# Perceiver block on one core: the last chunk of the cross attention gets a ring of five exp banks

## What is computed

```python
x = x + xattn(layernorm(x), ctx)          # the change is at the end of this one
x = x + attn(layernorm(x))                # 16 heads of 64
x = x + ffn(layernorm(x))                 # 16 experts, 4 chosen, and a shared one

def xattn(q, c, w_q, w_kv, w_concat):
    qh = (q @ w_q).reshape(B, L, 16, 16).transpose(0, 2, 1, 3)
    k, v = split(c @ w_kv)
    p = softmax(einsum('bhid,bjd->bhij', qh, k) / 4)
    return merge_heads(einsum('bhij,bjd->bhid', p, v)) @ w_concat
```

## Time and profile before

| | |
|---|---|
| median of 3 runs | 604.72 us (599.29 to 612.70) |
| the profiled execution | 603.77 us, of which the profile's span is 602.0 us |
| granted TensorE clock, mean | 0.99 |
| TensorE, VectorE, ScalarE, GpSimd busy | 93%, 77%, 67%, 20% of the span |
| where the last chunk lies | scores of its first tiles at 372.36 us, the product behind its loop at 395.50 us |

### The profile page before, as it was taken

The page is one execution under the profiler, slowest core; times in us unless marked ns, Lnnn a source line. Parts: engine busy times, 40 slices in busy tenths (PEclk is TensorE's granted clock), DMA queues, the critical chain, the costliest instruction groups (busy, mean ns, idle before and its releaser), DMA issues.

```text
span 602.0 us, 11657 instructions
## 1 busy us (share of the span) xinstructions
PE 558.3 (93%) x4488; PEld 301.6 (50%) x4488; DVE 464.7 (77%) x683; ACT 400.8 (67%) x814; POOL 121.9 (20%) x158
## 2 busy tenths in 40 slices
PE   2788999999999999999999999898999987989996
PEld 0353343344334433433443343356766765968885
DVE  5797997999999999999999994615445558695565
ACT  1326887888888888888888888753556553335441
POOL 5000000000000000000000000402366552177852
PEclk9989999999999999999999999998999999899999
DMA  8864200000122100000000000100050030032101
GB/s 314 216 121 127 79 25 25 25 26 26 34 52 69 44 1 1 1 2 2 1 2 2 1 1 1 36 2 17 19 175 28 10 105 2 1 97 88 50 5 35
DMA packets 19482, 28.09 MB, mean 47 GB/s; under 512 B 5570, under 2 KB 13316, under 8 KB 18404
## 3 DMA queue, kind: packets, MB, share of 16 engines
q1 hardware_dynamic: 19428, 27.35, 16.1%
HBM read 20.78 MB, written 0.52 MB: 35 GB/s over the span
## 4 chain that ended last, share of the span: by engine, by line
PE 73%; DVE 19%; ACT 3%; issue 3%; DMA 2%; SPq 0%; DVEq 0%
PE bank L658 23%; PE bank L669 19%; DVE mxp L1232 11%; PE pairS L747 5%; PE pairS L911 5%; PE bank L929 3%; PE pairS L797 3%; PE bank L824 2%; PE bank L911 2%; PE bank L810 2%; DMA ctx<-ctxT 2%; ACT Pb L1024 2%; PE bank L601 2%; PE pairS L677 1%; DVE Pb L1314 1%
## 5 line engine op out<-in xcount | busy, mean ns | idle before, releaser
L1232 DVE TENSOR_REDUCE mxp<-pairS 128x1 f32<-128x1024 f32 x256 | 308.2, 1222 | 20.3 <-PE pairS L652 19.2
L1024 ACT ACTIVATE Pb<-bank 128x512 f32<-128x512 f32 x512 | 278.2, 597 | 47.1 <-PE bank L658 23.8
L658 PE MATMUL bank<-qparts,kparts 64*128 64x512 f32 x512 | 184.2, 447 | 9.2 <-DVE mxp L1232 2.9
L652 PE MATMUL pairS<-kparts,qparts 64*128 64x512 f32 x512 | 183.5, 451 | 4.5 <-DVE mxp L1232 3.4
L669 PE MATMUL bank<-Pb,V 128*32 128x256 f32 x2048 | 160.3, 390 | 1.2 <-ACT accS L1010 1.2
L658 PEld LDWEIGHTS bank<-qparts,kparts 64*128 64x128 f32 x512 | 75.7, 184 | 109.1 <-ACT Pb L1024 59.9
L669 PEld LDWEIGHTS bank<-Pb,V 128*32 128x32 f32 x2048 | 42.0, 108 | 87.6 <-issue 47.2
L652 PEld LDWEIGHTS pairS<-kparts,qparts 64*128 64x128 f32 x512 | 75.4, 186 | 10.1 <-DVE mxp L1232 5.8
L466 POOL CAST mparts<-mneg 128x8 fp32r<-128x8 f32 x16 | 3.1, 196 | 350.3 <-DVE mneg L1240 350.3
L1303 DVE TENSOR_REDUCE smx<-pairS 128x2 f32<-128x512 f32 x32 | 21.8, 687 | 30.5 <-PE pairS L797 30.5
L481 POOL TENSOR_TENSOR Pb<-Pb,srd 128x512 f32<-128x512 f32 x32 | 33.3, 1039 | 56.5 <-DVE srd L1308 56.1
(11 more groups left out here) (187 smaller groups left out, 705.3 us busy)
## 6 DMA issues: line engine op xcount, KB each, us to landing
ctx<-ctxT SPq DMA_DIRECT2D x4, 2048.0 KB, 10.7
wU<-w_up SPq DMA_DIRECT2D x18, 256.0 KB, 2.9
wD<-w_down SPq DMA_DIRECT2D x18, 128.0 KB, 2.4
wA<-w_qk SPq DMA_DIRECT2D x8, 256.0 KB, 2.7
qparts<-qh SPq DMA_DIRECT2D x120, 16.0 KB, 1.8
wO<-w_out SPq DMA_DIRECT2D x8, 128.0 KB, 2.1
kparts<-kvh SPq DMA_DIRECT2D x32, 32.0 KB, 2.0
wV<-w_v SPq DMA_DIRECT2D x2, 512.0 KB, 4.5
```

The source lines that it names most:

```text
L652: last = mm(dst[:, i * 512:(i + 1) * 512], qparts[rows, at:at + P], kparts[c // NCH][rows, k:k + 512], start=True, stop=True)
L658: mm(dst[:], kparts[g // NCH][rows, s * P:(s + 1) * P], qparts[rows, g * CW:(g + 1) * CW], start=True, stop=True).then_inc(exp_filled, 1)
L1024: A(PT[:, s % 8, :], src, ACT.Exp, scale=1.0 / np.sqrt(XD)).then_inc(exp_free, 1)
L1232: nc.vector.reduce_max(mxp[:, c % 2 * NBLK + blk, kp:kp + 1], pairS[n % 2][:], AX).then_inc(max_free, 1)
```

## The change

Five edits, all in the last chunk (g = 15) and just behind it:

- The ring of exp banks gets two more, the halves of `pairS0` (`LAST`, `last_bank`, `LAST_RING` = 5). The first three tiles take banks as before, tiles 3 and 4 wait until VectorE has read the last row maxima, and every later tile n waits for the exp of tile n - 5.
- The product with V is issued for both sides at once, at s % 4 == 3 (`AT_ONCE`), and no longer in two halves.
- The transposed sums of chunk 14 go to the second half of `OFF` (`pairS1`), since `pairS0` is taken. VectorE reads them ahead of `close(0)`, where it read them behind it. The closing product of batch 0 uses the same half, so it now waits for that reading (`max_free` at its full count).
- The closing product moves from tile 8 to tile 12 (TensorE; 13 on VectorE), and the transposes of the normed batch 0 from tile 20 to 24 (25 on VectorE). The first transposes stay at tile 2.
- Behind the loop the first value tile comes ahead of q and k, and q and k wait for the exps of tiles 28 and 29, whose banks they take. The wait for `max_free` that stood there is gone.

```diff
--- before.py
+++ after.py
@@ -110,6 +110,9 @@
 
 EXP_TURN, MAX_TURN = turns()
 
+LAST_RING = 5
+CLOSE_AT, MEAN_AT, PARTS_AT = 2, 13, 25
+
 
 
 BY_BATCH = 3
@@ -175,6 +178,9 @@
         ACC = bank[2]
         MISC = bank[3]
         EXP = [bank[0], bank[1], MISC]
+        max_pair_of_sums = MAX_TURN["sums", NCHUNK - 2] % 2
+        LAST = [EXP[(EXP_TURN["s", NCHUNK - 1, 0] + i) % 3] for i in range(3)] + [
+            pairS[max_pair_of_sums][:, i * 512:(i + 1) * 512] for i in range(2)]
         XB = [bank[0], bank[1]]
         OFF = pairS[(MAX_TURN["sums", NCHUNK - 2] + 1) % 2]
         half = [pairS[0][:, 0:512], pairS[0][:, 512:1024], pairS[1][:, 0:512], pairS[1][:, 512:1024]]
@@ -569,6 +575,16 @@
                     have(AT_TURN[n - 3])
                 return EXP[n % 3]
 
+            def last_bank(s):
+
+                if s < 3:
+                    return exp_bank(("s", NCHUNK - 1, s))
+                if s < LAST_RING:
+                    pe.wait_ge(max_free, MAX_TURN["sums", NCHUNK - 2])
+                else:
+                    have(("s", NCHUNK - 1, s - LAST_RING))
+                return LAST[s % LAST_RING]
+
             def max_bank(what):
                 n = MAX_TURN[what]
                 if n >= 2:
@@ -707,14 +723,18 @@
             pe.wait_ge(dve_const, 1)
             for g in range(NCHUNK):
                 for s in range(KT):
-                    if s == SUMS_AT and g:
+                    if s == SUMS_AT and 0 < g < NCHUNK - 1:
                         sums(g - 1, max_bank(("sums", g - 1))).then_inc(max_filled, 1)
-                    if s == 2 and g == NCHUNK - 1:
-                        close_T(0)
-                    if s == 8 and g == NCHUNK - 1:
-                        close_product(0)
-                    if s == 20 and g == NCHUNK - 1:
-                        norm_batch_T(3, 0, OFF)
+                    if g == NCHUNK - 1:
+                        if s == CLOSE_AT:
+                            close_T(0)
+                        if s == SUMS_AT:
+                            sums(g - 1, OFF[:, 512:1024]).then_inc(max_filled, 1)
+                        if s == MEAN_AT - 1:
+                            pe.wait_ge(max_free, len(MAX_TURN))
+                            close_product(0)
+                        if s == PARTS_AT - 1:
+                            norm_batch_T(3, 0, OFF)
                     for what in BETWEEN.get((g, s), ()):
                         turn_of[what[0]](*what[1:])
                     if s == 0:
@@ -722,7 +742,7 @@
                     have(("ks", g // NCH, s // 4))
                     ahead = pair_at(g, s)
                     if g == NCHUNK - 1 and s % 2 == 0:
-                        here, there = exp_bank(("s", g, s)), exp_bank(("s", g, s + 1))
+                        here, there = last_bank(s), last_bank(s + 1)
                         scores(g, s, here, FOR_EXP)
                         scores(g, s + 1, there, FOR_MAX)
                     elif g < NCHUNK - 1:
@@ -732,7 +752,7 @@
                         scores(g, s, dst, FOR_EXP)
                         if ahead:
                             max_half(*ahead, s % 2, pair, FOR_MAX)
-                    for side in (APART if g == NCHUNK - 1 else SIDES_AT[s // 4]).get(s % 4, ()):
+                    for side in (AT_ONCE if g == NCHUNK - 1 else SIDES_AT[s // 4]).get(s % 4, ()):
                         if s >= 4:
                             weighted(g, s // 4 - 1, side)
                         elif g:
@@ -840,11 +860,12 @@
                    skip_group_check=True)
 
             first, second = slice(0, L), slice(L, 2 * L)
-            pe.wait_ge(max_free, len(MAX_TURN))
             pe.wait_ge(xl_done, 1)
+            values(("v", 0, 0), SB[0])
+            have(("s", G - 1, 28))
             rows_of(0, 0, PJ[0][:, first], first, q_ps)
+            have(("s", G - 1, 29))
             rows_of(0, 1, PJ[1][:, first], first, k_ps)
-            values(("v", 0, 0), SB[0])
             for side in range(2):
                 weighted(G - 1, QUADS - 1, side)
             values(("v", 0, 1), SB[1])
@@ -963,6 +984,8 @@
             def filled(what):
                 n = EXP_TURN[what]
                 act.wait_ge(exp_filled, n + 1)
+                if what[0] == "s" and what[1] == NCHUNK - 1:
+                    return LAST[what[2] % LAST_RING][:]
                 return EXP[n % 3][:]
 
             def x_move(b):
@@ -1269,20 +1292,21 @@
                     low_part(what)
             for g in range(NCHUNK):
                 for s in range(KT):
-                    if s == 2 and g == NCHUNK - 1:
+                    if s == CLOSE_AT and g == NCHUNK - 1:
                         oT_move()
                         for i in range(2):
                             high(wAh[i], wA[i], wA_in[i], wA_hi)
+                    if s == MEAN_AT and g == NCHUNK - 1:
                         close(0)
                         for i in range(2):
                             high(wVh[i], wV[i], wV_in[i], wV_hi)
-                    if s == 20 and g == NCHUNK - 1:
+                    if s == PARTS_AT and g == NCHUNK - 1:
                         x_parts(OFF[:, 0:512])
                         TS(bq8[:], bqkv[:, 0, :], 1.0 / np.sqrt(AD), None, ALU.mult).then_inc(bq_done, 1)
                     if s == SUMS_AT and g:
                         n = MAX_TURN["sums", g - 1]
                         dve.wait_ge(max_filled, n + 1)
-                        sums_rows(g - 1, pairS[n % 2], max_free)
+                        sums_rows(g - 1, OFF[:, 512:1024] if g == NCHUNK - 1 else pairS[n % 2], max_free)
                     for what in BETWEEN.get((g, s), ()):
                         if what in HALVED:
                             low_part(what)
```

## The result

The changed kernel takes 601.27 us (median of 20 runs, 594.52 to 607.66), the kernel before 604.08 us (median of 20). The ratio is 0.993 with a 95% interval of 0.9906 to 0.9954: about 4.2 us less, and the interval says 2.8 to 5.7. That is within 2%, a small gain that is clear of no change. The ratio leaves out the slow executions, those over 1.5% above the fastest of their kernel (four of the changed kernel's twenty), and so it says more than the 2.8 us between the two medians. Forecast were 3.6 us less, and 600.2 us from the profiled execution or 601.1 us from the median of three.

The account below looks back on a forecast made before the run. It took a loop of latencies between TensorE and ScalarE, neither full, as the bound; the loop ending at 391.89 instead of 395.50 saves 3.6 us, so 603.77 - 3.6 = 600.2 us (601.1 from the median), range 596.5 to 605.5.

Parts of the forecast that it names:

- The last chunk is a loop of latencies, and two more banks break it: Last chunk: TensorE and ScalarE wait in turn with three banks; five cut a quad from 2.43 us to 2.00 us.
- The loop ends at 391.89: End of the last chunk's loop: TensorE reaches the stage behind at 391.89 instead of 395.50, 3.6 us saved.
- One exp per 0.50 us; the bound of 0.60 us: ScalarE in the last chunk: one exp per 0.50 us; at 0.60, from 14 exps in 8.46 us, only 2.3 us saved.
- rival 1: Last chunk: ScalarE is the slower engine at 0.60 us per exp, giving 601.5 us; chance 0.14.
- The wait for the copy of `accS` stays at 0.9 us: TensorE ahead of the new accumulator's first product: a wait of 0.9 us stays, in place of 1.23.
- The new wait of the closing product costs nothing: Closing product, waiting for VectorE's sums: they end at 379.2, ahead of 379.99; costs nothing, 0.4 us at the upper bound.
- ScalarE still stands 1.7 us there: ScalarE at the closing product: it stands idle for 1.7 us, not 2.24.
- Margins of the moved steps: Norm, low tile and split of x are ready before TensorE asks, by 0.9, 2.0 and 2.2 us.
- Behind the loop the order costs nothing, and the gain is carried over whole: Behind the loop: the same 18 matmul rows take 3.01 us in another order, and the 3.6 us saved reaches the end.
- rival 3: Stages behind the loop: a load or GpSimd holds them, no gain comes out, time stays at 603.8 us; chance 0.07.
- Rival 2: Division of the sums: GpSimd holds it up to 1.48 us longer, saving 3.0 us, 600.8 us in all; chance 0.07.
- Rival 4: Last chunk's loop: TensorE's clock falls to half, up to 11.7 us slower, 615.5 us; chance 0.03.

Follow-up runs that it names:

- the four corners: Four kernels, three or five banks, each with halved or whole products with V; last-chunk stage 23.11 and 24.73 us with three, 21.73 and 19.29 with five.
- mean9: Changed kernel with the closing product at tile 8, right behind the sums, and the transposes at tile 20: 604.98 us in one run.
- ring3: Changed kernel with the last chunk's ring back to three banks, products still whole: 606.72 us, ratio 1.0072 to the kernel before.
- apart: Changed kernel, five banks, with the product with V again in two halves per quad: 605.32 us, ratio 1.0002 to the kernel before.
- early: Changed kernel, closing product moved into the `accS` copy wait, transposes to tile 16, sums to tile 20: 601.94, then 598.93 us; ratios to before 0.9964, 0.9893.
- acc4: Changed kernel with ScalarE copying chunk 14's `accS` one tile sooner, ahead of the exp of tile 4: 601.20 us, ratio 0.9925 to the kernel before.
- early2: Kernel early with whole products also in the last two quads of chunk 14: ratio 0.994 to the kernel before, stage 18.39 us.
- port: Changed kernel with VectorE's casts of `wA` right ahead of the sums' three steps, so GpSimd's subtractions meet the division: 601.65 us in one run.

## Why the prediction was right

Point by point, with the step as it was put and the row after:

- *The last chunk is a loop of latencies, and two more banks break it.* Shown by the four corners: with five banks the stage falls by 1.4 us with halves and by 5.4 us with whole products (24.73 to 19.29). One reading of the rows was loose: TensorE's two waits of 0.21 and 0.20 us belong to two quads, one each, and not to one.
- *The loop ends at 391.89.* It ended at 391.88, though the chunk had begun 0.23 us later, at 372.59. The stage was reckoned at 19.53 us and took 19.29, so the term was 0.24 us too long, and that the end fits to 0.01 us is luck. The term that was mis-sized are the scores: two pairs directly behind each other take 0.67 us (378.38 to 379.05), where 2 x 0.43 had been taken. TensorE was busy for 18.05 us and not 18.44, and idle for 1.24 us, where 1.09 had been reckoned.
- *One exp per 0.50 us; the bound of 0.60 us.* It was 0.478 us in the run of eleven, and rival 1 has fallen. The 14 exps in 8.46 us were no bound of ScalarE's own. Before, TensorE issued their scores only once per 1.23 us, two at a time, beside the row maxima, and that is 0.61 us for an exp:

```profile
362.43 0.49 PE L658 MATMUL bank<-qparts,kparts 64*128 64x512 f32 x1
...
363.66 0.49 PE L658 MATMUL bank<-qparts,kparts 64*128 64x512 f32 x1
...
364.89 0.49 PE L658 MATMUL bank<-qparts,kparts 64*128 64x512 f32 x1
```

- *The wait for the copy of `accS` stays at 0.9 us.* It was 1.03 us. The copy came at 376.06, where 375.81 had been reckoned, by the later start alone; TensorE was through 0.12 us earlier than reckoned from that start, by the cheaper scores, and waited that much longer.
- *The new wait of the closing product costs nothing.* The division ended at 379.41 (reckoned 379.2) and the product started at 380.05, straight behind the product with V. mean9 shows what it costs without the four tiles: 1.01 us of waiting and a stage 1.4 us longer.
- *ScalarE still stands 1.7 us there.* It stood for 1.52 us.
- *Margins of the moved steps.* `xn` was there at 386.78 (386.63 reckoned) and TensorE asked at 387.61; the first low tile of `wV` by about 390.2 (389.86 reckoned) and TensorE asked at 391.88. Nothing was late.
- *Behind the loop the order costs nothing, and the gain is carried over whole.* 3.01 us with q and k first and 3.02 with the value tile first. The stage behind is 7.72 us and was 7.71, so rival 3 has fallen as it was put. Here stays a rest: the stage gained 3.85 us, and at the same granted clock the end gained 3.4, with an error of about 0.2. For ring3, apart and early the two agree within 0.2 us; for acc4 the end gained 0.3 us less than the stage and for early2 0.6. No run settles where these went, or whether they are scatter.
- *Rival 2, GpSimd holding the division.* It did not happen, by the margin reckoned; port shows that it can, and that it is worth 0.4 us at this place.
- *Rival 4, the clock falling inside the loop.* In every stage row of this study the granted clock in the last chunk is 1.00, in the closer packed kernels as well. It falls elsewhere.
- *How the runs scatter.* The prediction took the 13.4 us between three runs as scatter and widened its range for it. No clock is on record for those three; over the later executions nearly all of such scatter goes with the granted clock. The range itself was not summed as described: halves of 5.4 and 8.0 us around 600.2 and 601.1 give 597.5 to 605.1, and 596.5 to 605.5 was written. The measured 601.27 lies in both. The base of the forecast, one profiled execution at a clock of 0.990, lay 1 us under what the kernel takes at 0.985.

## What to carry to other kernels

Where two engines hand tiles to each other and neither is full, add up the round trip (start to result, instruction, release) for the number of buffers there is, and compare it with each engine's own work per round; more buffers pay until the larger of the two works is reached. Here, with three banks, each pair of scores waited for an exp of the pair before it: 0.51 us from the scores to the exp and 0.74 from the exp to the released bank, 1.25 us for two tiles, against 1.00 us of TensorE's work (0.93 with whole products) and 0.96 of ScalarE's. With five banks the same 1.25 us are for four tiles. Issuing the product in one piece paid only once that loop was broken. Two edits may need each other: here whole products cost 1.6 us with three banks and brought 2.4 us with five. When times of single executions scatter more than the change is worth, read the stage in the trace and compare whole times at the same granted clock, and look as well whether the kernels' mean clocks differ, since that part the comparison takes out.

## What the runs showed of the hardware

- **Nearly all scatter goes with the granted clock.** Its mean lay between 0.975 and 1.000 over 142 executions of seven kernels: 448 us per unit, 0.8 us left over. In the traces it fell to 1.2 GHz in stretches at the start of the kernel, in the stage behind the last chunk, between the second and third block and at the very end. The profile of early has 10.2 us of it behind the last chunk (length, busy times of the engines, clock, DMA share, GB/s):

```profile
409.50:419.70 10.20, 9.57 (x32) 6.80 (x31) 3.32 (x6) 2.40 (x7) 1.95 (x3) 0.50 0.10 26
```

  In the kernel before, the stretch at 413.00 followed 9.79 us at full clock in which TensorE was busy for 8.11. In the profile after there is none in that stage, whose work is the same from the end of the loop on. Whether such a stretch comes is not decided by the program alone: the changed kernel's own executions range from 0.975 to 0.997.
- **An exp of 128 x 512 from PSUM costs ScalarE 0.478 us when nothing holds it** (eleven from 382.50 to 387.76 in the profile after), though its row is 0.60 to 0.73 us long: in a long run the rows overlap, and their durations grow while the distance from start to start stays the same.
- **Two pairs of 64-row scores directly behind each other cost TensorE 0.67 us** (378.38 to 379.05 in the profile after), a pair by itself 0.43 us (390.91 to 391.34 before).
